# At most two gathers of rows in flight on two semaphores, in the edge stage of a graph transformer

## The reference

```python
k_j, q_i, v_j = (k[src], q[dst], v[src])
kw = rel_apply(k_j, etype, Watt)
a = (kw * q_i).sum(-1) * pri[:, etype].T / SQRT_D
amax = jax.ops.segment_max(a, dst, num_segments=n)
ex = jnp.exp(a - amax[dst])
den = jax.ops.segment_sum(ex, dst, num_segments=n)
alpha = ex / (den[dst] + 1e-16)
m = rel_apply(v_j, etype, Wmsg)
agg = jax.ops.segment_sum(alpha[..., None] * m, dst, num_segments=n)
```

## Time and profile before

| | |
|---|---|
| runs of the kernel | 3336.67, 3383.07 and 3389.13 us, median 3383.07 us |
| the profiled execution, its span | 3418.8 us |
| busy in it: DVE, PE, POOL, ACT | 2154.3, 2097.2, 1947.8, 1534.9 us |
| gathers of the edge stage on POOL (L1242) | 1564 of 945 ns, 1478.4 us |
| all DMA | 511.26 MB, mean 150 GB/s |

### The profile page before, as it was taken

The page is one execution under the profiler, slowest core; times in us unless marked ns, Lnnn a source line. Parts: engine busy times, 40 slices in busy tenths (PEclk is TensorE's granted clock), DMA queues, the critical chain, the costliest instruction groups (busy, mean ns, idle before and its releaser), DMA issues. The chain is left out here.

```text
span 3418.8 us, 52858 instructions
## 1 busy us (share of the span) xinstructions
PE 2097.2 (61%) x12592; PEld 1812.6 (53%) x12592; DVE 2154.3 (63%) x5522; ACT 1534.9 (45%) x5149; POOL 1947.8 (57%) x2030
## 2 busy tenths in 40 slices
PE   2567726666666666666566626666666666666565
PEld 1455515556566555655444525556655555555544
DVE  6576527666666666666555626666666666666577
ACT  0015514444444444544555614444444444444554
POOL 4415555666666666666355564666666666666265
PEclk6568867776767777677677866776777767777655
DMA  5416655555555555555245554555555555555321
GB/s 125 80 74 262 274 159 143 152 154 157 154 153 153 154 155 151 156 154 152 71 188 200 218 161 141 148 153 155 152 155 155 154 157 156 153 153 151 111 56 31
DMA packets 386069, 511.26 MB, mean 150 GB/s; under 512 B 75321, under 2 KB 298235, under 8 KB 373268
## 3 DMA queue, kind: packets, MB, share of 16 engines
q0 software_dynamic: 101952, 326.75, 30.8%
q1 hardware_dynamic: 274712, 179.39, 17.9%
q10 hardware_dynamic: 9104, 1.86, 0.3%
HBM read 382.63 MB, written 142.96 MB: 154 GB/s over the span
## 5 line engine op out<-in xcount | busy, mean ns | idle before, releaser
L1242 POOL DMA_INDIRECT g_rows<-node_kv,edge_key_sb x1564 | 1478.4, 945 | 913.1 <-issue 415.8
L1412 ACT ACTIVATE acc<-g_ps_sum 128x127 f32 x1564 | 420.5, 269 | 691.9 <-issue 498.9
L1477 PE MATMUL g_ps_sum<-g_hot,g_rows 128*128 128x128 f32 x3128 | 597.1, 348 | 163.5 <-ACT acc L1416 118.0
L1496 PE MATMUL g_ps_q<-g_qw,g_hot_t 128*128 128x128 f32 x3128 | 629.6, 372 | 106.7 <-DVE g_rows L1268 43.5
L1416 ACT ACTIVATE acc<-acc,g_gained,g_scale x1564 | 601.1, 384 | 136.0 <-issue 120.5
L1477 PEld LDWEIGHTS g_ps_sum<-g_hot,g_rows 128*128 128x128 f32 x3128 | 545.1, 259 | 203.7 <-ACT acc L1416 138.2
L1496 PEld LDWEIGHTS g_ps_q<-g_qw,g_hot_t 128*128 128x128 f32 x3128 | 586.6, 282 | 119.5 <-issue 58.0
L1522 PE MATMUL g_ps_a<-g_ends,head_of_row 112*8 112x56 f32 x224 | 38.0, 270 | 551.9 <-DVE g_alpha L1303 461.9
L1485 PE MATMUL g_ps_hot<-ident,g_hot_t 128*128 128x128 f32 x1564 | 310.9, 325 | 50.6 <-issue 29.0
L1268 DVE TENSOR_TENSOR g_rows<-g_rows,g_ps_q 128x512 f32<-128x512 f32 (+1 forms) x446 | 263.3, 608 | 118.2 <-remote 85.2
L1522 PEld LDWEIGHTS g_ps_a<-g_ends,head_of_row 112*8 112x8 f32 x224 | 13.5, 88 | 576.1 <-issue 576.1
(11 more groups left out here) (247 smaller groups left out, 3204.1 us busy)
## 6 DMA issues: line engine op xcount, KB each, us to landing
g_qw<-node_q SPq DMA_DIRECT2D x1564, 64.0 KB
g_rank_row<-edge_rank SPq DMA_DIRECT2D x110, 448.0 KB
g_rows<-node_kv,edge_key_sb POOLq DMA_INDIRECT x1564
node_agg<-n_agg SPq DMA_DIRECT2D x24, 256.0 KB, 2.3
node_rows<-node_x SPq DMA_DIRECT2D x2, 1792.0 KB
node_q<-l_blank_q SPq DMA_DIRECT2D x1, 3200.0 KB
node_q<-n_q_sb,node_slot POOLq DMA_INDIRECT x112
node_kv<-n_kv,node_id POOLq DMA_INDIRECT x112
```

The source lines that it names most:

```text
L1242: g_.indirect_dma_start(out=rows[b % U][:, g, :], out_offset=None, in_=scratch["kv"][:, :], in_offset=bass.IndirectOffsetOnAxis(ap=tab["ke ...
L1412: a.activation(acc[:, bass.ds(w + 1, P - 1)], ps_sum[q % 2][:, n, 1:P], ACT.Copy).then_inc(s["copied"], 1)
L1477: ins = t.matmul(ps_sum[q % 2][:, n, :], rows[b % U][:, g, D:2 * D], hot[b % U][:, g, :], start=True, stop=True)
L1496: ins = t.matmul(ps_q[q % 2][:, n, :], hot_t[b % 2][:, g, :], qw[b % 2][:, g, :], start=True, stop=True)
```

## The change

GpSimd now waits, ahead of every gather but the first two of a layer, until the gather two before it has landed, so that at most two are in flight. They raise two semaphores in turn, by the parity of the tile's number, instead of six. `landed(tile, u)` is what semaphore u stands at when all gathers of its parity up to `tile` have landed. VectorE waits ahead of every group's products for both semaphores, up to the last tile of that group, instead of for eight tiles ahead of the first group and six ahead of the third. The waits on `sums` and the row buffers stay as they are, and so does all else.

```diff
--- before.py
+++ after.py
@@ -1137,6 +1137,7 @@
 
 
 FOUR = 4
+IN_FLIGHT = 2
 EDGE_TILES = -(-E // P)
 SIZES = (G,) * (B - 1) + (EDGE_TILES - (B - 1) * G,)
 BATCHES = len(SIZES)
@@ -1156,7 +1157,6 @@
 
     q_in = [s[f"q_in{u}"] for u in range(2)]
     ranks_in = [s[f"ranks_in{u}"] for u in range(2)]
-    EARLY = 8
     with ExitStack() as st:
         sb = lambda n, sh, d=F32: st.enter_context(nc.sbuf_tensor(f"g{l}_{n}", sh, d))
         pb = lambda n, sh: st.enter_context(nc.psum_tensor(f"g{l}_{n}", sh, F32))
@@ -1195,9 +1195,9 @@
 
             return tuple(b - n if 0 <= b - n < BATCHES else None for n in range(3))
 
-        def loaded(b, late):
-
-            return 16 * sum(max(n - EARLY, 0) if late else min(n, EARLY) for n in SIZES[b % U:b + 1:U])
+        def landed(tile, u):
+
+            return 16 * len(range(u, tile + 1, IN_FLIGHT))
 
         def windows(engine, regs, b, g):
             if g == 0:
@@ -1239,8 +1239,10 @@
                         if g % FOUR == 0 and b >= U:
                             pool.wait_ge(s["sums"], GROUP[b - U] + g // FOUR + 1)
                         at = FIRST[b] + g
+                        if at >= IN_FLIGHT:
+                            pool.wait_ge(rows_in[at % IN_FLIGHT], landed(at - IN_FLIGHT, at % IN_FLIGHT))
                         g_.indirect_dma_start(out=rows[b % U][:, g, :], out_offset=None, in_=scratch["kv"][:, :],
-                                              in_offset=bass.IndirectOffsetOnAxis(ap=tab["key"][:, at:at + 1], axis=0)).then_inc(rows_in[2 * (b % U) + (g >= EARLY)], 16)
+                                              in_offset=bass.IndirectOffsetOnAxis(ap=tab["key"][:, at:at + 1], axis=0)).then_inc(rows_in[at % IN_FLIGHT], 16)
 
                 over(batch, 0)
 
@@ -1259,10 +1261,8 @@
 
                 def products(b, k):
                     four = FOURS[b][k]
-                    if k == 0:
-                        dve.wait_ge(rows_in[2 * (b % U)], loaded(b, False))
-                    if k * FOUR == EARLY:
-                        dve.wait_ge(rows_in[2 * (b % U) + 1], loaded(b, True))
+                    for u in range(IN_FLIGHT):
+                        dve.wait_ge(rows_in[u], landed(FIRST[b] + four[-1], u))
                     half = rows[b % U][:, four[0]:four[-1] + 1, 0:D]
                     dve.wait_ge(s["spread"], GROUP[b] + k + 1)
                     v.tensor_tensor(half, half, ps_q[(GROUP[b] + k) % 2][:, 0:len(four), :], ALU.mult).then_inc(s["prod"], 1)
@@ -1582,7 +1582,7 @@
             if l == 0:
                 early.close()
                 acc = sb("acc", [P, NP])
-            edge_stage(nc, c, edges, own(f"edges{l}_rows_in", 2 * U), nodes, l, tab, scratch, acc, weights)
+            edge_stage(nc, c, edges, own(f"edges{l}_rows_in", IN_FLIGHT), nodes, l, tab, scratch, acc, weights)
         node_stage(nc, c, nodes, put, edges, L, tab, scratch, acc, weights, out)
```

## The result

Beside each other the kernel before took 3379 us and the changed one 3851 us, 1.141 times as long (95% interval 1.135 to 1.147). The profiled execution has a span of 3843.5 us, 424.7 more than before. The forecast was 3560 us; the sign was right, but a batch grew by 4.5 us where the sum had 1.6.

A forecast was written before the change was run, and what follows sets the result against it. GpSimd's own gather sequence, 21.03 us a batch with two gaps, was taken as the bound. To the 3418.8 us span the cap added 170 and the heads 13: 3602 us, about 3560 at the median's scale; range 3240 to 3720.

The forecast's parts named there:

- 2.82 us a pair: GpSimd's gathers: landing at 2.55 us plus 0.27 to resume, instead of 2.50 a pair; +1.60 us a batch.
- faster rival: GpSimd's gathers: TensorE's signals come in time, both gaps go, 19.74 us a batch, 3260 us; chance 0.27.
- I take 2.55 to the semaphore: Gather's DMA queue: last packets in 2.3 to 2.5 us after the start, semaphore taken at 2.55 us.
- upper bound of 0.59: GpSimd's resumption, high value for the range: 3.14 us a pair, +3.20 us a batch, 3744 us.
- There is room: SyncE's slices of `q` beside the gathers: DMA share 0.55, and thinner gathers leave more room.
- Both gaps kept: GpSimd ahead of tiles 0 and 8: gaps stay while pairs slow, +1.6 us a batch; chance 0.38.
- The heads: First 42 gathers of each layer: 20 pairs at 0.32 us more, +13 us for both layers.
- Much slower: GpSimd, once blocked, resumes only when everything in flight has landed: 28.5 us a batch, 4235 us; chance 0.08.
- one at a time: GpSimd: a wait plus a semaphore change drains at every gather, 39.5 us a batch, about 5450 us; chance 0.04.
- Finer waits on VectorE at nothing: VectorE's products: 6 more waits a batch on long satisfied semaphores, covered by 6.35 us idle; cost taken as nothing.

The follow-up runs named there:

- no-ranks run: The changed kernel without the broadcast of the ranks after the first batch: 3688 us against the changed kernel's 3852.
- finer-waits kernel: The kernel before, without a cap, but VectorE waits ahead of each group's products for that group's gathers only, on twelve semaphores: 2808.9 us, 0.9987.

## Why the prediction was wrong

The step that failed is the price of a gather that is held back: 2.82 us a pair, from a semaphore at 2.55 us and 0.27 us of resumption. Measured, it is 3.01 us with one wait, 3.49 with two, and 4.8 beside the broadcast. With seven pairs of 2.82 and no gap a batch is the 19.74 us of the prediction's faster rival; 25.5 were measured. The 5.8 us between them go as follows.

**The landing was 0.20 us too short.** "I take 2.55 to the semaphore", it says; the last packet is in at 2.41, but the semaphore reaches its count at 2.75. The resumption behind it was right: 0.27 from the row on which TensorE's sums release GpSimd, and 0.26 behind a landing, if the gather carries one wait. So a pair costs 3.01 (0.19 more), 1.3 us a batch over seven pairs. The upper bound of 0.59 would have given 3.14.

**The stacked wait was not in the sum, and it is the largest term.** Four gathers a batch carry the sums' wait as well; they resume 0.74 us after the landing, 0.48 later: 1.9 us a batch. Before, a satisfied wait at tiles 4 and 12 cost nothing, since GpSimd wasn't held back there; the prediction kept that wait at nothing without asking what it costs beside one that holds.

**The slow landing was taken as hidden.** "There is room" was said of the transfers. In the kernel before the last packet of the gather beside the broadcast is in at 3.4 us, and nobody waits for it. With two in flight the next pair does: tile 10 lands at 4.07 instead of 2.75, 1.3 us a batch (1.5 in the no-ranks run).

**The sum as measured**: 7 × 3.01 = 21.1, + 4 × 0.48 = 1.9, + 1.3 for the broadcast, is 24.3. Tiles 0, 2 and 12 land at 3.05, 3.06 and 2.93; beside them SyncE's slices of `q` move 103 to 126 KB (from 1.4 to 2.7 us after their start), beside tiles 4, 6 and 8, which land at 2.73 to 2.75, nothing. That adds 0.8: 25.1. The last 0.4 us of the mean of 25.5 are not accounted for, and no run left the slices out.

**"Both gaps kept" failed too, in the other direction.** The drains vanished from the edge stage. The forecast added pauses to gaps; the runs fit the longer of two chains, 25.5 us by the cap or 21.0 by whatever makes the gaps. In the sessions without gaps 25.6 stands against 17.5, and the same change costs 31%. So the forecast had only five pairs and two gaps where the kernel has seven pairs and none; that error made up for part of the others.

**The heads gave 16 us instead of costing 13.** The late signals went there too: the changed kernel has no wait on "remote" left in its edge stages. Two of VectorE's waits in the head of the kernel before:

```profile
486.44 0.69 DVE L1268 TENSOR_TENSOR g_rows<-g_rows,g_ps_q 128x512 f32<-128x512 f32 x1 [15.04 <-remote]
505.52 1.02 DVE L1268 TENSOR_TENSOR g_rows<-g_rows,g_ps_q 128x512 f32<-128x512 f32 x2 [16.46 <-remote]
```

TensorE ended the first group of sums 85.3 us after the first gather there and 61.7 us in the changed kernel, so its 43rd gather no longer waits for them as in the 31.55 us of the earlier trace rows.

**The rivals.** The faster one was half right: late signals went from the edge stage and the time did not follow. Much slower (28.5 us a batch) and one at a time (39.5) did not come. Finer waits on VectorE at nothing was right without the cap and 2.4% off beside it; the place of the broadcast explains that, by the landings of tiles 10 to 12.

## What to carry to other kernels

A cap on transfers in flight is free only if (number in flight) × (issue spacing) exceeds the slowest landing plus the issuer's resumption, with the waits that it really carries; here 2 × 1.25 = 2.5 stood against 3.0 to 4.8 us; with four it was 5.0 against at most 4.9 (4.15 and 0.74), and a cost of 1.0% or less was left. Count the landing to the semaphore and not to the last packet. Price a new wait from a place where the issuer is held by the same kind of thing, count the waits already standing at that instruction, and look for the one slow transfer in each period that nobody yet waits for. Where a stage has idle gaps of its own, compare the two chains whole instead of adding to one.

## What the hardware showed beyond that

A gather that is held back by a landing starts 0.26 us after the semaphore with one wait and 0.74 with two, even if the second was satisfied long ago; not held back, the same second wait shows no cost (1.25 us from start to start at tiles 4 and 12 of the kernel before).

In some sessions TensorE's semaphores themselves move late. In the kernel before that of the transposed scores (L1508) moved more than 0.5 us after the end of the transposition in 106 of 112 cases, 2.9 us after it in the median. It moved when the last packet of the gathers under way had landed (0.04 us after that in the median, most within 0.15), and VectorE's scan started 0.02 us behind the semaphore. So what the prediction inferred from the earlier trace rows is what the trace records, for 106 scans rather than all 112. In the finer-waits kernel at 2809 us the same semaphore moved 0.01 us after the end.

The prologue shows the same two kinds. VectorE's L571 waited there, first in the kernel before at 3384 us, then in the finer-waits kernel at 2809 us:

```profile
  remote: 38.3, 10
```
```profile
  PE e_ps_h L640: 8.6, 27
```

A chip that had the late signals in one session (3418 us) had none in a later one (2813 us). They cost the kernel before 570 to 610 us, of which some 430 in the edge stages (1193.7 and 1191.2 us from first to last gather against 980.2 and 977.4).

The number in flight switches them in the edge stage, within the slower kind of session: with three in flight 104 of 111 recorded moves of that semaphore were late, with two none of the 54 that the trace recorded (58 are missing from it), with one none at all. Of the recorded moves of the sums' semaphore with two in flight 310 of 315 were on time as well. So at least where the trace has a record, the cap of two did not only hide the late signals behind VectorE's waits for gathers. Why they depend on the stream of gathers, and what makes one session differ from another, is open.
